# Final experts of a two-layer gated block: loads of all eight at once, norms one expert ahead

## What is computed

```
x = x + tanh(g_xattn[0]) * attention16heads(layernorm(x), ctx, mask)
x = x + tanh(g_ffn[0])   * expert_choice_ffn(layernorm(x))       # 8 experts, top 512 tokens each
x = x + tanh(g_xattn[1]) * bidirectional_attention(layernorm(x), ctx)
x = x + tanh(g_ffn[1])   * first_choice_experts(layernorm(x))    # 8 experts, capacity 512
```

```
probs = softmax(xt @ wg); idx = argmax(probs); mask = one_hot(idx) * (location < C)   # C = 512
exp_out = einsum('ech,efh->ecf', exp_in, W) + b
out = gate * exp_out at each token's place, 0 for a token that was dropped
```

## Time and profile before

| | us |
|---|---|
| median of the 3 runs (779.02 to 782.97) | 780.43 |
| the profiled execution's own time | 787.23 |
| its span, first to last instruction | 785.5 |
| PE busy in it | 675.3 |
| POOL busy in it | 260.7 |
| final stage, from SyncE's first load | 722.60 to 785.5 |

### The profile page before, as it was taken

The page is one execution under the profiler, slowest core; times in us unless marked ns, Lnnn a source line. Parts: engine busy times, 40 slices in busy tenths (PEclk is TensorE's granted clock), DMA queues, the critical chain, the costliest instruction groups (busy, mean ns, idle before and its releaser), DMA issues.

```text
span 785.5 us, 14749 instructions
## 1 busy us (share of the span) xinstructions
PE 675.3 (86%) x5303; PEld 463.8 (59%) x5303; DVE 425.5 (54%) x1290; ACT 328.0 (42%) x703; POOL 260.7 (33%) x377
## 2 busy tenths in 40 slices
PE   5999998999999984864999999997599999993773
PEld 3565654555555553642666666656478888872663
DVE  5645546677778755784222222112368887673544
ACT  2343434777776771523222222220645555411640
POOL 4101102334443432005345545233101343244465
PEclk9999998899999997976999999999699999996997
DMA  8669943566665215952254694325313472123661
GB/s 265 197 180 244 261 117 89 99 131 128 132 120 130 65 58 168 95 181 70 35 123 93 165 321 99 65 27 125 117 55 108 144 249 98 58 75 109 193 200 65
DMA packets 105040, 103.12 MB, mean 131 GB/s; under 512 B 22102, under 2 KB 95321, under 8 KB 104964
## 3 DMA queue, kind: packets, MB, share of 16 engines
q1 hardware_dynamic: 95752, 85.72, 42.1%
q0 software_dynamic: 9216, 16.46, 9.4%
HBM read 60.15 MB, written 42.25 MB: 130 GB/s over the span
## 4 chain that ended last, share of the span: by engine, by line
PE 38%; DVE 6%; issue 5%; ACT 4%; DMA 4%; POOL 2%; SPq 0%; another core or an unknown queue 0%; POOLq 0%; DVEq 0%; ACTq 0%
PE pc L1486 9%; PE pc L1463 9%; PE pc L950 3%; PE pc L2013 2%; PE pc L2006 2%; DMA g_rows<-scratch_slots 1%; PE pc L1482 1%; PE pc L2004 1%; PE pc L2073 1%; ACT enc L1865 1%; PE pc L1466 1%; PE pc L2286 1%; PE pc L1450 1%; PE pc L1973 1%; DVE d_w_c L1782 1%
## 5 line engine op out<-in xcount | busy, mean ns | idle before, releaser
L617 ACT ACTIVATE probs<-pb,b_key_cols 128x512 f32<-128x512 f32 x128 | 92.8, 779 | 17.0 <-PE pb L787 17.0
L484 DVE TENSOR_REDUCE neg_max<-pb 128x4 f32<-128x512 f32 x128 | 81.7, 680 | 3.0 <-PE pb L767 3.0
L1366 POOL DMA_INDIRECT scratch_resid<-y,k_idx x32 | 54.7, 1708 | 86.1 <-DVE y L1416 85.8
L1434 ACT ACTIVATE mid<-pc,b_up 128x512 f32<-128x512 f32 x40 | 27.4, 687 | 112.8 <-PE pc L1463 109.9
L1486 PE MATMUL pc<-w_dn,mid 128*128 128x256 f32 x320 | 73.3, 384 | 0.0
L1463 PE MATMUL pc<-gT,w_up 128*128 128x512 f32 x160 | 71.5, 603 | 0.9 <-DVE gT L1398 0.9
L1486 PEld LDWEIGHTS pc<-w_dn,mid 128*128 128x128 f32 x320 | 59.5, 190 | 12.7 <-issue 5.3
L1463 PEld LDWEIGHTS pc<-gT,w_up 128*128 128x128 f32 x160 | 31.0, 194 | 36.9 <-issue 36.5
L1416 DVE TENSOR_SCALAR y<-pc,gate 128x256 f32<-128x256 f32 x32 | 15.5, 484 | 65.1 <-PE pc L1486 47.2
L1357 POOL DMA_INDIRECT rows<-scratch_rows,k_idx x32 | 31.2, 975 | 57.8 <-DVE k_idx L1240 48.4
L365 POOL CAST nm_parts<-neg_max 128x16 bf16<-128x16 f32 x32 | 6.3, 198 | 125.4 <-DVE neg_max L484 125.4
(11 more groups left out here) (342 smaller groups left out, 1424.1 us busy)
## 6 DMA issues: line engine op xcount, KB each, us to landing
qs<-scratch_qparts SPq DMA_DIRECT2D x48, 128.0 KB, 4.5
ks<-scratch_kparts SPq DMA_DIRECT2D x48, 128.0 KB
w_dn<-in_W_down SPq DMA_DIRECT2D x8, 640.0 KB
scratch_slots<-s_zero SPq DMA_DIRECT2D x1, 4160.0 KB, 20.6
c_in<-in_ctx SPq DMA_DIRECT2D x8, 512.0 KB, 6.7
s_x<-in_x SPq DMA_DIRECT2D x8, 512.0 KB, 7.1
scratch_ctxT<-cT SPq DMA_DIRECT2D x8, 512.0 KB, 6.4
scratch_resid<-s_x SPq DMA_DIRECT2D x16, 256.0 KB, 3.1
```

The lines of the kernel that those rows point to most:

```text
L484: V.tensor_reduce(neg_max[:, h:h + 4], ps_s[b][:].rearrange("p (h k) -> p h k", h=4), AX.X, ALU.max, negate=True).then_inc(max_s, 1)
L617: A.activation(probs[2 * u + b][:], ps_st[b][:].rearrange("p (h q) -> p h q", h=4), ACT.Exp, bias=key_cols[:, 1, t:t + 1], scale=key_cols[ ...
L1366: pool.indirect_dma_start(out=T["resid"], out_offset=bass.IndirectOffsetOnAxis(ap=S["idx"][:, e, c:c + 1], axis=0), in_=y[e % 2][:, c, :], ...
```

## The change

All loads of the final stage are issued in a row with no wait between them; rows, weights and biases have eight places each (`rows`, `w`, `bias` are indexed by e, not e % 4), and experts 4 and 5, and 6 and 7, share one semaphore for their six loads. These semaphores are taken over from an earlier part (`aside`), so their counts start from what that part left. Expert 0's rows come in three loads: chunk 0, chunk 1, chunks 2 and 3. VectorE norms the chunks of expert 0 as they come, and the first two chunks of expert 1 too, behind chunk 0's result. ScalarE norms chunks 2 and 3 of expert 1, and then for each pair of an expert copies the turned pair and norms the same pair of the next expert. The indices of expert 0 are made in three instructions, and GpSimd waits for the indices ahead of each scatter. WARM is 12.

```diff
-    ST, WARM = CAP // P, 14
+    ST, WARM = CAP // P, 12
-    rows, xn = [sb(f"g_rows{i}", [P, ST, ROW1]) for i in range(4)], ...
+    rows, xn = [sb(f"g_rows{i}", [P, ST, ROW1]) for i in range(EXPERTS)], ...
+    w = S["w_1"] + [sb(f"g_w{i}", [P, HALVES, D]) for i in range(4, EXPERTS)]
+    bias = S["b_1"] + [sb(f"g_b{i}", [P, D]) for i in range(4, EXPERTS)]
+    second_s, others_s, others_in = sem("pg_rest"), aside.room_in[0], 16 * (aside.LOADS[0] + 1)
+    late_s = {4: aside.room_in[1], 6: aside.cT_in[0]}
+    late_in = {4: 16 * (aside.LOADS[1] + 6), 6: 16 * (QUADS // 2 + 6)}
+    def loaded(engine, e):
+        if e < 4:
+            engine.wait_ge(in_s[e], 48)
+        else:
+            engine.wait_ge(late_s[e // 2 * 2], late_in[e // 2 * 2])
     def weights(sp, e):
-        if e >= 4:
-            sp.wait_ge(y_s, (e - 3) * ST)
...
     def on_sync(sp):
         sp.wait_ge(bidir.sent_s, 16 * TILES)
+        sp.dma_start(rows[0][:, 0:1, :], slots_t[:, 0:1, :]).then_inc(in_s[0], 16)
+        sp.dma_start(rows[0][:, 1:2, :], slots_t[:, 1:2, :]).then_inc(second_s, 16)
+        sp.dma_start(rows[0][:, 2:ST, :], slots_t[:, 2:ST, :]).then_inc(others_s, 16)
+        for e in range(1, 4):
+            sp.dma_start(rows[e][:], slots_t[:, e * ST:(e + 1) * ST, :]).then_inc(in_s[e], 16)
+        for e in range(4, EXPERTS):
+            weights(sp, e)
+            sp.dma_start(rows[e][:], slots_t[:, e * ST:(e + 1) * ST, :]).then_inc(late_s[e // 2 * 2], 16)
     def on_gpsimd(pool):
...
-            pool.wait_ge(idx_s, e + 1)
             for c in range(ST):
+                pool.wait_ge(idx_s, min(c, 2) + 1 if e == 0 else e + 3)
                 pool.wait_ge(y_s, e * ST + c + 1)
...
     def on_scalar(act):
+        def norm(e, first, end):
+            loaded(act, e)
+            if e == 1:
+                act.wait_ge(xn_s, ST + first)
...
-        norm(1)
-        norm(2)
+        norm(1, 2, ST)
         for e in range(1, EXPERTS):
             for j in range(2):
+                turned_out(e, j)
+                if e + 1 < EXPERTS:
+                    norm(e + 1, 2 * j, 2 * j + 2)
-            if e + 2 < EXPERTS:
-                norm(e + 2)
     def on_vector(dve):
...
-        norm_first()
-        index(0)
-        for c in range(ST):
+        norm(0, 0)
+        index(0, 0, 1)
+        norm(0, 1)
+        index(0, 1, 2)
+        norm(0, 2)
+        norm(0, 3)
+        index(0, 2, ST)
+        chunk(0, 0)
+        norm(1, 0)
+        norm(1, 1)
+        for c in range(1, ST):
             chunk(0, c)
```

More of the change, by code:

```diff
@@ L2151, in bidirectional_stage, with first_choice_stage @@
                  bias_on_vector=bias_on_vector, sent_s=sent_s, stored_s=stored_s)
-def first_choice_stage(nc, S, T, sem, sb, ps, bidir):
-    ST, WARM = CAP // P, 14
+def first_choice_stage(nc, S, T, sem, sb, ps, bidir, aside):
+    ST, WARM = CAP // P, 12
     two = lambda n, s, d=F32: [sb(f"{n}{i}", s, d) for i in range(2)]
-    rows, xn = [sb(f"g_rows{i}", [P, ST, ROW1]) for i in range(4)], [sb(f"g_xn{i}", [P, ST, D]) for i in range(3)]
+    rows, xn = [sb(f"g_rows{i}", [P, ST, ROW1]) for i in range(EXPERTS)], [sb(f"g_xn{i}", [P, ST, D]) for i in range(3)]
     rT = two("g_rT", [P, HALVES, CAP])
-    w, bias = S["w_1"], S["b_1"]
+    w = S["w_1"] + [sb(f"g_w{i}", [P, HALVES, D]) for i in range(4, EXPERTS)]
+    bias = S["b_1"] + [sb(f"g_b{i}", [P, D]) for i in range(4, EXPERTS)]
     yb = two("g_yb", [P, ST, D])
@@ L2208, in on_scalar, with turned_out @@
     def on_scalar(act):
-        def norm(e):
+        def norm(e, first, end):
+            loaded(act, e)
+            if e == 1:
+                act.wait_ge(xn_s, ST + first)
             if e >= 3:
                 act.wait_ge(t_ps, ST if e == 3 else turned(e - 3, 1))
-            act.wait_ge(in_s[e % 4], 48 * (e // 4 + 1))
-            for c in range(ST):
-                nc.scalar.activation(xn[e % 3][:, c, :], rows[e % 4][:, c, 0:D], ACT.Identity, bias=rows[e % 4][:, c, D:D + 1],
-                                     scale=rows[e % 4][:, c, D + 1:D + 2]).then_inc(xn_s, 1)
+            for c in range(first, end):
+                nc.scalar.activation(xn[e % 3][:, c, :], rows[e][:, c, 0:D], ACT.Identity, bias=rows[e][:, c, D:D + 1],
+                                     scale=rows[e][:, c, D + 1:D + 2]).then_inc(xn_s, 1)
+        def turned_out(e, j):
+            act.wait_ge(t_ps, turned(e, j))
+            if e >= 2:
+                act.wait_ge(y_ps, (e - 2) * ST + 2 * j + 2)
+            nc.scalar.activation(rT[e % 2][:, :, 2 * j * P:2 * (j + 1) * P], ps[e % 2 * 2 + j][:].rearrange("p (h t) -> p h t", h=HALVES),
+                                 ACT.Copy).then_inc(rT_s, 1)
         for c in range(ST):
@@ L2233, in on_vector @@
-    def on_vector(dve):
[L2234 to L2243, removed]
+                turned_out(e, j)
@@ new lines, in on_scalar, with norm, index @@
+                if e + 1 < EXPERTS:
+                    norm(e + 1, 2 * j, 2 * j + 2)
+    def on_vector(dve):
+        def norm(e, c):
+            if e == 0:
+                dve.wait_ge(*((in_s[0], 48), (second_s, 16), (others_s, others_in), (others_s, others_in))[c])
+            else:
+                loaded(dve, e)
+            nc.vector.tensor_scalar(xn[e][:, c, :], rows[e][:, c, 0:D], rows[e][:, c, D + 1:D + 2], rows[e][:, c, D:D + 1],
+                                    ALU.mult, ALU.add).then_inc(xn_s, 1)
+        def index(e, first, end):
+            if e:
+                loaded(dve, e)
@@ L2264, in pair @@
                 result(e, c)
-        norm_first()
-        index(0)
-        for c in range(ST):
+        norm(0, 0)
[9 more added lines that the diff above has]
+        for c in range(1, ST):
             chunk(0, c)
-        index(1)
+        index(1, 0, ST)
         for e in range(1, EXPERTS):
@@ L2274, in on_vector @@
             if e + 1 < EXPERTS:
-                index(e + 1)
+                index(e + 1, 0, ST)
     def on_tensor(pe):
@@ L2307, in pair @@
             if j == 0:
-                pe.wait_ge(in_s[e % 4], 48 * (e // 4 + 1))
+                loaded(pe, e)
             if e >= 2:
```

33 lines of the change are left out of this document (10 added, 23 removed).

## The result

Before 781.4 us (median of 6 runs, 778.28 to 783.47), after 776.06 us (6 runs, 775.29 to 776.9): ratio 0.9935, 95% interval 0.9909 to 0.9962. The change gains 5.3 us where 8.7 were forecast, and 776.06 lies 0.6 above the range.

A forecast was written before the change was run, and what follows sets the result against it. The prediction took POOL's scatters, 1.28 us apart with gaps blamed mostly on late loads, to bound the final stage. Earlier first rows and nearly gapless scatters gave 8.7 us less: 771.7 us, range 769.0 to 775.5.

The forecast's parts named there:

- What bounds the kernel: Final stage: POOL's 32 scatters at 1.28 us each set the pace; POOL lost 8.9 us, mostly in three gaps.
- Who made y late?: Final stage: blamed late y on ACT's four waits for rows of experts 4 to 7, 8.5 us in total.
- Sum: Final stage: last scatter at 770.9 against 779.62, 8.7 us less; taken off the median 780.43 this gives 771.7.
- Loads at once: Final stage's loads: all eighteen issued by about 731, all in by 744.3; no stall at experts 4 to 7.
- First rows by chunks: Expert 0's rows: separate chunk loads let the first scatter start at 730.08 instead of 731.02, 0.94 us gained.
- Norms one ahead: ScalarE's norms by halves: chunk 1's scatter 0.44 us behind POOL's pitch, expert 1's first scatter 0.3 behind it.
- Fewer warm-ups, split indices: Stage start: twelve warm-ups end 0.4 us earlier without gain; POOL's second wait per scatter costs 0, bounds 0 and 1.6 us.
- Rival 1: PE's clock rises late, behind the dense work after 727.7: 2.3 us lost, gain 6.4 us, 774.0; chance 0.12.
- a granted clock of 0.50 behind 727: Sign on PE's clock in the final stage, listed among those that would show the forecast wrong.
- Rival 2: Late experts' loads stay as slow as now, 8.4 us per 904 KB: 0.3 us gained, 780.1; chance 0.05.
- Rival 3: PE's clock stays at 1.2 GHz, 8.66 us an expert, so PE bounds: 19 us slower, 799.4; chance 0.03.

The follow-up runs named there:

- e3: The kernel before with all eight experts' loads issued at once into eight places, nothing else changed: 781.08 us, ratio 1.0007 to before.
- e4: The kernel after with the loads of experts 4 to 7 put back behind before's waits for results: 776.53 us, ratio 0.996 to before.
- e11: The kernel before with no loads at all for experts 4 to 7, same amount of work: 789.16 us, ratio 0.9994 to before.
- e1: The kernel before, unchanged, profiled a second time, on chip 7: 780.76 us, ratio 1.001 to before.
- e14: The kernel after with 32 more warm-up transposes on PE ahead of its wait, on chip 13: ratio 0.9943 to before.
- e2: The kernel after, unchanged, profiled a second time, on chip 7: 776.83 us, ratio 0.9954 to before.
- e8: The kernel after with 390 KB more read ahead of each late expert's loads, on chip 8: 785.51 us, ratio 0.9975 to before.
- e9: The kernel before, unchanged, profiled again on chip 12: 789.44 us, ratio 1.0006 to before.

## Why the prediction was wrong

**What bounds the kernel.** POOL's pitch was read rightly: 1.28 before and after, under load too. The gap ahead of 739.46 was rightly the stage's order. The step that failed is "Who made y late?". There I took the list's 8.5 us of ACT's waits for rows as the reason of the gaps at 751.59 and 767.99, because the norm of 742.78 had waited and its expert's scatters came late. A wait's total says that an engine waited, not that anything behind it did. e3, e4 and e11 show that those waits lay inside PE's lead, and e1 that such waits (6.2 us) come without those gaps. So the loads' part of the sum, the five us of those two gaps, measured nothing. The rows that would have told were in the trace of before:

```profile
745.38 1.99 PE L2286 MATMUL pc<-w,g_rT 128*128 128x256 f32 x8 [1.16 <-ACT g_rT L2228]
...
748.03 2.08 ACT L2214 ACTIVATE g_xn<-g_rows 128x256 f32<-128x256 f32 x4 [2.21 <-DMA g_rows<-scratch_slots]
...
749.52 0.69 DVE L2260 TENSOR_TENSOR g_yb<-pc,b 128x512 f32<-128x512 f32 x1 [3.94 <-PE pc L2286]
...
751.59 0.97 POOL L2201 DMA_INDIRECT result<-g_y,g_idx  x1 [2.19 <-DVE g_y L2249]
```

The late scatter of 751.59 stands on DVE's addition of 749.52, whose product was done at 747.37, 2.15 us earlier. No load and no norm lies between the two. The addition of 765.99, ahead of 767.99, is of the same kind: its product (758.14) was done at 760.03, and DVE had been free since 761.88.

**Sum.** A step of 8.7 us was read from one profiled execution and applied to a median 6.8 us below that execution. Its late starts were part of why it was slower: 1.89 + 3.10 = 5.0 us, and where they are absent before's stretch is 50.99 (its first scatter is 0.84 earlier too). From there the same sum, 48.3, would have given a gain of 2.7 us and 777.7. That the first profile of after met the sum (48.53) is the part of it that was right, POOL's pitch and the order; that this profile also lay 8.5 us of stretch under before's, as forecast, is luck: the execution of before that was profiled had the late starts. The same chips give 3.3 us of stretch (50.99 to 47.68, chip 7) and 2.4 (56.54 to 54.13, chip 12). The difference of the two first profiles, 11.9 us, holds 8.5 of this stretch; another 3.5 came ahead of it, for the first load was issued at 719.09 and not 722.60, where the two kernels are alike.

**Loads at once.** The forecast of the traffic was about right (all in by 744 forecast, which is 21.7 us after the first load, and 740 to 742 measured, which is 20.9 to 22.9; no wait for rows in the first profile of after). SyncE's eighteen issues took 13.9 us where 8.4 were forecast, since they grow longer (below), and nothing waited for them. The value of the loads was wrong: they have none.

**First rows by chunks.** In direction right: 0.94 us forecast, 7.58 to 6.97 = 0.61 measured on chip 7, 7.73 to 6.67 = 1.06 on chip 12. With the late clock it is 8.42 to 7.78 between the first profiles.

**Norms one ahead.** Right, and it is the gain: expert 1's gap falls from 3.01 to 0.63 (0.3 forecast). Chunk 1's was put at 0.44 and is 0.16 here (0.47 and 0.58 in e4 and e14). The order and the first rows were never run one without the other on a chip free of late starts, so their shares of the 3.3 us are read from the gaps.

**Fewer warm-ups, split indices.** POOL's second wait costs nothing seen: scatters that wait for nothing keep 0.30. Whether 14 warm-ups would make late rises of the clock rarer wasn't tried; in seven profiles of before and its variants it rose at 2.8 to 4.0 us, and in ten with the stage of after and its 12 warm-ups at 2.9 to 3.8 seven times and at 5.9 to 6.1 three times.

**Rival 1** came true in part. The clock did rise late, in three of those ten profiles, before and not behind the stage's dense work, and it cost about 0.9 us of stretch (48.53 to 48.63 against 47.36 to 47.82), not 2.3. That was a sign named in the prediction, a granted clock of 0.50 behind 727: the rise 5.9 us after the first load is 728.5 on before's scale. In the first profile of after PE worked from 719.12 and the clock stayed at 0.50 to 725.0; in e2, with PE begun as early, it rose 2.8 us sooner. The Trainium skill (TensorE: Matmul & The Clock Gate, Part 1) has activity release the throttled state: the traces agree, and it doesn't tell these two starts apart.

**Rival 2** didn't occur: loads and scatters together moved 373 GB/s, and the scatters kept 1.28. The Trainium skill's turn-taking of queues (DMA: Bandwidth & Descriptors, Queues, rings and completion order) may hold beside that; no run here shows a cost from it. **Rival 3** didn't occur.

**The rival that was missing**: the late loads are covered already and the gaps have another cause. I had it in my own numbers, 4.33 against 5.12 us, and used them only for the time after the change.

**Still open**: why PE's increments come late. The late starts keep their place (scatters 12 and 22) in before, in after, with no late loads and with 120 more PE instructions, take others with the extra loads (10 and 18 in e8), and they go by the chip, as far as one group of runs on each of four chips can tell chip from hour. Nothing here shows their cause. Also open is whether they make up the rest of the difference between chips (before's medians 780.0, 780.8, 787.9 and 790.0, of which the stretch holds 5.6 of the 10 between chips 7 and 12), and why the ratio was lower with the runs of chip 13 and the first comparison than with those of chips 7, 8 and 12. The intervals overlap, some of them barely.

## What to carry to other kernels

An engine's wait is worth nothing until it is followed, row by row, to the late instruction of the engine that bounds the stage; and where a gap's releaser was long done, look for when its semaphore was incremented before blaming the engine that waited. Before a step read from one profiled execution is taken off a median, profile the kernel a second time on another chip and see which gaps stay. Where a faster producer already leads its consumer, prefetching earlier brings nothing: e4, with the waits back and thus free to keep four places, is as fast as the change.

## What the runs showed of the hardware

- Late starts: behind the gaps over 1.4 us, DVE began 2.1 to 5.3 us after PE's product was done by the trace and DVE was free. It began 0.09 us or less after the increment of PE's semaphore, so the increment was late. Two chips' profiles all have such gaps, two others' none. Between e1 and e9, both before, they are 56.54 - 50.99 = 5.6 us of the stage.
- One kernel's median differs by 1.3% from chip to chip (780.0 and 790.0), about twice the whole change, so only runs on the same chip compare.
- SyncE's issues grow longer when many loads are queued. In the kernel after, weights loads took, the first and the last:

```profile
722.04 0.75 SPq L2184 DMA_DIRECT2D g_w<-in_W  x1
...
728.99 1.98 SPq L2184 DMA_DIRECT2D g_w<-in_W  x1
```

Alone it took 0.37. Nothing waited behind them here, but an urgent load behind such a row would.
- TensorE's granted clock rose from 1.2 to 2.4 GHz between 2.9 and 6.1 us from the stage's first load in kernels whose start is the same.
